# A routed feed-forward kernel: last scatters spread over sixteen pages, results sent eighteen pages behind, slot work in three pieces

## The reference, cut to what matters

```python
x = x + conv_block(ln_over_channels(x))          # sign convolutions 2x3, batch norm, relu; x is 16 x 64 x 32 x 32
t = tokens(x)                                     # 16384 tokens of 64 numbers
n = ln(t)
probs = softmax(n @ gate_w + gate_b); two of 16 experts, weights renormalised
t = t + sum over the two experts of weight * ((silu(n @ w1[e]) * (n @ w2[e])) @ w3[e])
```

## Time and profile before

| | us |
|---|---|
| median of three runs (least, most) | 602.46 (601.66, 604.95) |
| the profiled execution, its own time | 599.37 |
| its span | 597.6 |

### The profile page before, as it was taken

The page is one execution under the profiler, slowest core; times in us unless marked ns, Lnnn a source line. Parts: engine busy times, 40 slices in busy tenths (PEclk is TensorE's granted clock), DMA queues, the critical chain, the costliest instruction groups (busy, mean ns, idle before and its releaser), DMA issues.

```text
span 597.6 us, 14183 instructions
## 1 busy us (share of the span) xinstructions
PE 494.6 (83%) x4186; PEld 432.2 (72%) x4186; DVE 440.2 (74%) x1242; ACT 394.9 (66%) x946; POOL 288.6 (48%) x378
## 2 busy tenths in 40 slices
PE   5899996896987427179599999999999999989962
PEld 5566775674665315179489999999899989989952
DVE  4577586685789696078278888888888898888853
ACT  4686884675675202077288888888787878878750
POOL 4000036666667675634744455545454444445461
PEclk8887897997979565679879999999999999999986
DMA  7941101011000012132122222233142324310213
GB/s 280 298 85 36 36 13 58 29 58 61 25 26 27 25 33 64 41 69 53 39 55 54 48 45 43 55 61 80 41 121 56 109 56 119 86 36 15 102 61 141
DMA packets 62663, 40.97 MB, mean 69 GB/s; under 512 B 50003, under 2 KB 54318, under 8 KB 62080
## 3 DMA queue, kind: packets, MB, share of 16 engines
q1 hardware_dynamic: 52208, 23.84, 17.5%
q0 software_dynamic: 8800, 8.94, 4.5%
q10 hardware_dynamic: 1584, 7.29, 3.2%
HBM read 21.46 MB, written 19.19 MB: 68 GB/s over the span
## 4 chain that ended last, share of the span: by engine, by line
PE 41%; DVE 21%; issue 12%; ACT 12%; another core or an unknown queue 6%; DMA 3%; SPq 2%; POOL 1%; DVEq 0%; ACTq 0%; POOLq 0%
PE up L963 7%; PE up L965 6%; PE up L795 5%; PE turn L979 4%; PE lines L996 4%; ACT xc L695 3%; DVE hidden L1580 3%; DVE xs_lo L1505 2%; DMA x_in<-in_x 2%; PE small L811 2%; PE small L840 2%; DVE hidden L1585 2%; PE lines L998 2%; ACT hidden_hi L708 2%
## 5 line engine op out<-in xcount | busy, mean ns | idle before, releaser
L511 POOL DMA_INDIRECT results<-result,page_in x147 | 153.6, 1045 | 148.9 <-ACT xc L695 89.0
L495 POOL DMA_INDIRECT pages<-payload,slot_int x128 | 128.9, 1007 | 143.5 <-DVE slot_int L1406 73.7
L963 PE MATMUL up<-up_w,xs_hi 128*128 x588 | 163.9, 310 | 19.9 <-DVE xs_lo L1505 13.7
L965 PE MATMUL up<-up_w,xs_lo 128*128 x588 | 150.5, 288 | 0.3 <-issue 0.3
L695 ACT ACTIVATE xc<-up 128x512 f32<-128x512 f32 x147 | 89.6, 609 | 79.2 <-PE up L965 32.0
L963 PEld LDWEIGHTS up<-up_w,xs_hi 128*128 128x128 f32 x588 | 114.3, 194 | 24.8 <-issue 21.8
L965 PEld LDWEIGHTS up<-up_w,xs_lo 128*128 128x128 f32 x588 | 115.2, 196 | 1.8 <-issue 1.8
L1580 DVE SCALAR_TENSOR_TENSOR hidden<-up,page_in,xc 128x128 f32<-128x128 f32 x196 | 59.2, 343 | 33.0 <-ACT xc L695 25.4
L1590 DVE TENSOR_TENSOR hidden_lo<-turn,hidden_hi 128x512 f16<-128x512 f32 x98 | 66.8, 681 | 8.2 <-ACT hidden_hi L708 8.1
L708 ACT ACTIVATE hidden_hi<-turn 128x512 f16<-128x512 f32 x98 | 61.4, 626 | 7.4 <-remote 7.4
L979 PE MATMUL turn<-ident,hidden 128*128 128x128 f32 x392 | 60.2, 277 | 5.2 <-DVE branch L1590 4.3
(11 more groups left out here) (262 smaller groups left out, 988.6 us busy)
## 6 DMA issues: line engine op xcount, KB each, us to landing
pages<-up_w ACTq DMA_DIRECT2D x4, 1332.0 KB, 10.1
page_in<-pages SPq DMA_DIRECT2D x147, 36.0 KB
page_in<-pages SPq DMA_DIRECT2D x147, 32.0 KB
x_in<-in_x SPq DMA_DIRECT2D x7, 512.0 KB
out<-up_raw SPq DMA_DIRECT2D x5, 512.0 KB
results<-result,page_in POOLq DMA_INDIRECT x147
up_raw<-in_L_ffn_w SPq DMA_DIRECT2D x4, 512.0 KB, 16.8
pages<-payload,slot_int POOLq DMA_INDIRECT x128
```

Of the source, the lines that this page charges most:

```text
L495: pool.indirect_dma_start(out=pages, out_offset=bass.IndirectOffsetOnAxis(ap=slot_int[q % PAYLOADS][:, t:t + 1], axis=0), in_=payload[q % ...
L511: pool.indirect_dma_start(out=results, out_offset=bass.IndirectOffsetOnAxis(ap=page_in[g % LOADS][:, k, D + AT_TOKEN:D + AT_TOKEN + 1].bit ...
L963: pe.matmul(target, xs_hi[g % 2][:, k * P:(k + 1) * P], weights[:, bass.ds(e * 2, 2 * HID)], start=True, stop=False)
L965: last = pe.matmul(target, xs_lo[g % 2][:, k * P:(k + 1) * P], weights[:, bass.ds(e * 2, 2 * HID)], start=False, stop=True)
```

## The change

GpSimd: the scatters of the pair before the last wait, from the fourth on, for `silu_done` 1 to 7, and the last pair's for 7 to 16 instead of 1 to 16. Each result n waits for `silu_done` of 18 + n up to n = 100, and of 118 + 3(n - 100)/4 beyond, at most 147. VectorE: `order_rows` comes ahead of the slot work of the pair at that step; the last pair's slot work is cut in three pieces that stand behind `hide(0)`, `hide(1)` and `hide(2)`; `make_low(2)` moves from step 9 of the 12 steps (0 to 11) to step 3. ScalarE: `make_hi(2)` moves up within step 3. TensorE: page 0's second product waits for the last slots, since both use the PSUM bank `lines`. `back_step` and SyncE's queue are as they were.

```diff
-                if q == PAIRS - 2 and t % 2:
+
+                if q == PAIRS - 2 and t == 1:
                     pool.wait_ge(rows_turned, 1)
+                if q == PAIRS - 2 and t >= 3:
+                    pool.wait_ge(silu_done, (t - 1) // 2)
                 if q == PAIRS - 1:
-                    pool.wait_ge(silu_done, 1 + t)
+                    pool.wait_ge(silu_done, 7 + 6 * t // 10)
...
+            def result_page(n):
+                turn = 100
+                return 18 + min(n, turn) + 3 * max(n - turn, 0) // 4
+
             for n in range(PAGES):
                 g, k = n // BY, n % BY
+                pool.wait_ge(silu_done, min(PAGES, result_page(n)))
                 if n >= LAST:
                     pool.wait_ge(result_ready, last_ready(n))
                 elif k == 0:
                     pool.wait_ge(result_ready, g + 1)
-                elif g < GROUPS - 3:
-                    pool.wait_ge(silu_done, min(PAGES, BY * (g + 2) + k + 1))
...
+                if t == 3:
+                    make_hi(2)
                 if t == 1:
                     act.wait_ge(dve_made, DM_ALL)
...
-                if t == 3:
-                    make_hi(2)
...
-                elif k == 0 and g:
+                elif n == 0:
+
+                    pe.wait_ge(slots_ready, PAIRS)
+                elif k == 0:
                     pe.wait_ge(result_ready, g)
...
+                if t == PAIRS + 2:
+                    order_rows()
                 if z == PAIRS - 1:
                     for k in range(8):
                         roster_step(0, k)
                     rows_low(0)
-                if z >= 0:
+                elif z >= 0:
+                    slot_rows(z)
+                    slot_ranks(z)
                     slots(z)
-                if t == PAIRS + 2:
-                    order_rows()
...
+                    if t == 3:
+                        make_low(2)
                     score(b)
...
                 if t == PAIRS + 1:
-                    make_low(2)
                     make_low(1)
...
                 if n < PAGES:
                     hide(n)
+
+                if n == 0:
+                    slot_rows(PAIRS - 1)
+                elif n == 1:
+                    slot_ranks(PAIRS - 1)
+                elif n == 2:
+                    slots(PAIRS - 1)
```

More of the change, by code:

```diff
@@ L1354, in weights, with each, slot_rows @@
                                   by_x[:, :, :], ALU.mult).then_inc(weights_placed, 1)
[L1358 to L1361, removed]
+            def each(a):
+                return a[:, :].unsqueeze(1).to_broadcast([P, TILES, LINES])
+            def slot_rows(q):
+                total = rank_ps[:, TILES, :]
                 was, now = begun[q % 2], begun[(q + 1) % 2]
@@ L1387, in slots, with slot_ranks @@
                 then(dve.tensor_tensor(base_new[:, :], offset[:, :], full[:, :], ALU.add))
+            def slot_ranks(q):
+                rank, total = rank_ps[:, 0:TILES, :], rank_ps[:, TILES, :]
                 settled(1)
@@ L1396, in slots @@
                 then(dve.tensor_tensor(base[:, :], base_old[:, :], base_new[:, :], ALU.add))
+            def slots(q):
                 settled(1)
```

## The result

The changed kernel took 633.71 us as the median of four runs (629.99 to 635.27), the kernel before on the same chip 602.06 (599.66 to 604.95): a ratio of 1.053, interval 1.050 to 1.057. The forecast of slower was right; the size, 611 in a range to 627, was not.

A forecast was written before the change was run, and what follows sets the result against it. TensorE sets the pace while pages flow; unbroken indirect transfers hold up other queues early. 599.37 - 20.6 - 3.1 - 2.5 + 31.5 + 3.6 = 608.3, plus 3.1 to the median: 611 us, range 594 to 627.

The forecast's parts named there:

- Part 4: TensorE's turns of pairs 0 to 3: result loads come 7.0 to 8.7 us late, 31.5 lost, plus 3.6 for clock.
- Rival D: Result loads aren't late because SyncE's queue order or the gate was misread: 576 us, chance 0.08.
- B: Faster: pacing wholly frees the page stage and SyncE's queue, so loads follow their pages quickly: 594 us, chance 0.12.
- Part 2: Last pages and results: 4.6 us back before the last silus, 1.5 lost behind them, net gain 3.1.
- the two gaps I had read: ScalarE idle 14.46 us before page 2's silu and 7.42 before a hidden_hi, while GpSimd issued unbroken indirect transfers.
- the sum (608.3): Profiled execution of the kernel before, 599.37 us, less the three gains, plus late loads and clock loss.
- Part 1: Pages 0 to 18: scatters and first results paced by silu take 46.1 us against 66.7, gain 20.6.
- the bound of 8.7: Lowest gain at the start: about four more held-up stretches of 3 us each, 58 us for 18 pages.
- one gap of 3.2: Pages 0 to 15: a single hold-up of 3.2 us added to 36.8 us of transfers, giving 40.0.
- rival C: Slower still: near unbroken scatters still hold up queues, or gaps have another cause: 623 to 632 us, chance 0.20.
- Part 3: Weight, order and slot work moved around the first pages: gain 2.5 us, bounds 0 and 4.5.
- The packet rule: DMA engines alternate between queues packet by packet, so pacing the scatters would bring nothing: 632 us.

The follow-up runs named there:

- gates_alone: Kernel before with only the change's gates for the results (18 pages behind, then four in three): 581.66 us, ratio 1.071.
- the dose: Changed kernel with results sixteen or thirteen pages behind instead of eighteen: 566.35 us (ratio 1.046) and 541.86 us (0.997).
- late_turns_again: Changed kernel with TensorE's turns of pairs 0 to 3 put 8 pages later, quick ground: 543.87 us, ratio 1.000 to the kernel before.
- late_turns_d: Changed kernel with TensorE's turns of pairs 0 to 3 put 8 pages later, slow ground: 593.36 us against 601.72 before, ratio 0.986.
- series_four_c: Kernel before with results 24 to 123 sent four at a time, slow ground: 647.27 us against 601.72 before, ratio 1.076.
- queue_as_before: Changed kernel with GpSimd's whole queue as in the kernel before, leaving only the moved weight work, order_rows and slot pieces: 541.24 us, ratio 0.999.
- changed_again: The changed kernel itself measured once more, on the quick ground: 583.73 us against 543.05 before, ratio 1.077.
- series_four_b: Kernel before with results 24 to 123 sent four at a time, quick ground: ratio 1.001 to the kernel before.

## Why the prediction was right, and where it wasn't

**Part 4, the late result loads: right.** Forecast were waits of 7.0, 8.7, 8.7 and 7.1, together 31.5; measured 6.7, 7.8, 7.6 and 8.2, together 30.4. With 0.9 each for the clock the forecast was 35.1; measured 37.6 with all that follows, on the profile's own ground, and 40.2 on the quick one. The order of SyncE's queue, the shift by nine pages and TensorE's fixed steps gave it, and gates_alone, the dose and late_turns_again show it by experiment on the quick ground; on the slow one late_turns_d has no such wait. Rival D falls with that, and B too: in the changed kernel the start gave back 9.9 and not 26.7, and the loads were no sooner behind their pages than before (7.99 against 7.87 for pair 0).

**Part 2, the end: the step that failed.** I counted "two results at most go with one page there" as harmless, because the two gaps I had read were behind series of ten. The step was "In the changed kernel two results at most go with one page there. That gives back 4.6", net 3.1 won, with no cost for the doubles in the sum. Measured: 3.0 won at pages 145 and 146 (5.75 us from page 144's silu to page 146's, where 4 to 5 was to be seen) and 1.6 lost behind the last silu against 1.5 forecast, but 11.9 lost on the way, in pages 118 to 144, where every third page has two results. Two transfers of 1.3 us in a page of 1.8 to 2.3 leave no pause, and series_four_c shows what a short series costs there; a run that takes these doubles alone away on the slow ground is missing. This one omission is 11.9 of the 27 us between the sum (608.3) and the profiled execution (635.17); part 1's size is 10.7 more. Neither alone puts the time outside the range: with the 11.9 alone the forecast 611.4 becomes 623, with both 634.

**Part 1, the start: mechanism right on the slow ground, size off.** Forecast 20.6, measured 9.9 to page 18, near the bound of 8.7 (13.3 in late_turns_d, which has the same code there, so single executions differ by some 3 us). The pacing wasn't tested alone on this ground: the three versions with it take 53.4 to 57.0 us for pages 0 to 18, the two without it 66.7 and 67.5. On the quick ground there was nothing to win. I had seen that 29 transfers of 1.27 us don't fit into 15 pages, and took one gap of 3.2; the trace has seven steps of 3.7 to 8.4 us (to pages 3, 5, 8, 10, 13, 16 and 18). That is rival C's way, "in many small gaps", and its time of 623 to 632 came nearest. I gave it 0.20. That it came so near is in good part luck: with the 9.9 measured, C's own reason gives 622, and the rest up to 634 is the cost of the doubles, which C didn't have either. One reading in the prediction was off without harm: the product done at 242.5 is page 3's, page 2's was done at 237.9, so that silu was held still longer with its product there.

**Part 3, the moved work: not confirmed.** 2.5 was forecast. In the profiled executions page 0 begins 1.8 earlier, but that place differs by 2 to 4 us between executions with the same front. On the quick ground queue_as_before has 0.999 with an interval (0.996 to 1.002) that allows no gain as well as 0.4%. One step was wrong there: "The three pieces go between hides in which VectorE waits for silu anyway". On the quick ground every version with the three pieces takes 38.8 to 39.0 us for pages 0 to 18, every version without them 37.3 to 37.4. The loss is in the step to page 4, 4.6 us: VectorE gets to the next group's low halves only behind the third piece, and TensorE waits for them. The row of changed_again from 209 to 249 us (who waits for whom, us in total, times, longest):

```profile
PE up L970 <- DVE xs_lo L1521: 3.0, 1, 3.0
```

queue_as_before has the same 3.0; without the pieces (series_four_b) this wait is 1.0.

**The packet rule** of the Trainium skill (DMA: Bandwidth & Descriptors, Queues, rings and completion order), by which the pacing should have brought nothing: the quick ground agrees with what I drew from it (series of four, 1.001), the slow ground does not (1.076), and there the measurement decides. It doesn't refute the rule itself: the rule is about the DMA engines' queues, and what stood in the rows above is ScalarE, with its product there.

**A range too narrow** came of both: it held no term for a pace above one transfer per page, on the only part of the kernel behind the scatters where the change sets such a pace, and it left out the upper half of C.

## What to carry to other kernels

When a wait is made longer, look up every fixed step that consumes its product, through all queues in between, and compare the added time with the slack in each: up to the slack it is free, beyond it is paid in full, on the engine that sets the pace. Catching up can cost too, as it did on the slow ground: ask of each stretch whether the queue that catches up still has a pause in every turn of the loop. And time a kernel before and after in one comparison; here the same kernel differed by a tenth from one to the next.

## What was not expected of the hardware

The two grounds. On the slow one, before took 598 to 602 us; on the quick one 542 to 543, and page 0's silu came at 207 to 214 us instead of 231 to 236. On the slow one unbroken series of indirect transfers hold ScalarE: it still starts some work behind the first transfers of a series, then mostly none until the series ends. On the quick one no such hold shows. Within a series the transfers take GpSimd as long on both (0.98 us, 0.30 apart). One chip showed both in different comparisons. What decides it, stays open: nothing in the views of the profile that I compared tells it, and no run varied it. By what way a series holds ScalarE is open too; shown is only that it does, with the average left alone and the clock at full, and that TensorE's matmuls went on in the series read closely.
